# A graph network on one core: edge attributes copied to PSUM ahead of the two statistics scans, and the second block's steps moved

## What is computed

```python
def _gat_layer(x, src, dst, W_i, a_src_i, a_dst_i, b_i):
    h = (x @ W_i).reshape(n, H, C)
    e = leaky_relu(es[src] + ed[dst])
    m = jax.ops.segment_max(e, dst, num_segments=n)
    p = jnp.exp(e - m[dst])
    alpha = p / segment_sum(p, dst)[dst]
    return segment_sum(alpha[:, :, None] * h[src], dst).reshape(n, H * C) + b_i
...
out1 = jax.ops.segment_sum(edge_attr, col, num_segments=n)
mx = jax.ops.segment_max(edge_attr, col, num_segments=n)
...
feat = jnp.concatenate([x, out1, out2, out3, u[batch]], axis=1)
```

## Time and profile before

| | |
|---|---|
| median of 3 runs | 9148.24 us (9145.92 to 9149.09) |
| span of the profiled execution | 9145.7 us |
| gathers of attention layer 1 (first to end of the last) | 2090.0 to 4271.4 us: 2181.4 us |
| layer 2 | 4421.3 to 6602.4 us: 2181.1 us |
| layer 3 (no statistics steps) | 6788.2 to 8929.0 us: 2140.8 us |
| busy share of the span | PE 62%, DVE 59%, POOL 58%, ACT 49% |

### The profile page before, as it was taken

How to read it: one execution, slowest core, us unless ns; L and a number is a source line. 1 busy time by engine, 2 the same in 40 slices (tenths; PEclk the granted TensorE clock), 3 DMA queues, 4 the chain that set the end, 5 groups by cost and what they waited for, 6 DMA issues and landing times.

```text
span 9145.7 us, 130431 instructions
## 1 busy us (share of the span) xinstructions
PE 5627.4 (62%) x34288; PEld 4519.0 (49%) x34288; DVE 5425.3 (59%) x12708; ACT 4499.0 (49%) x8146; POOL 5269.3 (58%) x5192
## 2 busy tenths in 40 slices
PE   4999879974555555555455555555534545445456
PEld 3777646653444454544344545454434444444444
DVE  6888731134666666666466666666645555555555
ACT  2555400014555555554455565555525555555554
POOL 2000100046777777775677777777657777777770
PEclk9999989965555555555555555555555555555558
DMA  3333335504444444443344444444423333333331
GB/s 99 140 139 135 134 131 190 190 8 117 121 118 122 116 125 116 120 119 91 87 121 116 124 116 125 115 121 119 107 64 81 86 81 86 81 86 81 86 81 32
DMA packets 601479, 989.13 MB, mean 108 GB/s; under 512 B 331106, under 2 KB 455043, under 8 KB 561523
## 3 DMA queue, kind: packets, MB, share of 16 engines
q0 software_dynamic: 163760, 357.05, 17.1%
q1 hardware_dynamic: 217540, 544.34, 16.9%
q10 hardware_dynamic: 219648, 81.82, 3.4%
HBM read 758.42 MB, written 224.34 MB: 107 GB/s over the span
## 4 chain that ended last, share of the span: by engine, by line
PE 34%; DVE 18%; DVEq 15%; issue 14%; POOL 13%; DMA 5%; ACT 1%; POOLq 0%; SPq 0%; ACTq 0%
PE bank L979 14%; DVEq L1284 13%; POOL arena L650 12%; PE bank L1202 8%; DVE acc L1882 8%; DMA arena<-row_table,staged_idx 4%; PE bank L1004 3%; PE bank L1130 2%; DVE arena L1838 2%; PE bank L1142 2%; DVEq L1882 1%; DVE arena L1869 1%; DVE x_mem L1556 1%; DVE arena L1831 1%; PE bank L1267 1%
## 5 line engine op out<-in xcount | busy, mean ns | idle before, releaser
L650 POOL DMA_INDIRECT arena<-row_table,staged_idx x4992 | 4982.4, 998 | 1622.7 <-issue 1490.7
L1202 PE MATMUL bank<-arena 128*128 128x136 f32 x9984 | 2504.4, 432 | 1193.0 <-DVE acc L1882 900.5
L1202 PEld LDWEIGHTS bank<-arena 128*128 128x128 f32 x9984 | 2211.2, 318 | 1378.6 <-issue 1372.7
L1882 DVE TENSOR_TENSOR acc<-acc,bank 128x136 f32 x4992 | 1476.6, 296 | 1062.5 <-issue 778.0
L806 ACT ACTIVATE pick_dist<-col,dst_local 128x128 bf16<-128x128 f32 x4992 | 1522.0, 387 | 293.0 <-issue 244.3
L979 PE MATMUL bank<-arena 128*128 128x385 bf16 (+1 forms) x7546 | 1342.6, 327 | 49.5 <-DVE arena L1660 33.0
L598 POOL TENSOR_TENSOR arena<-acc,node_stat 128x896 f32 x14 | 24.4, 1744 | 1730.4 <-POOLq L610 956.4
L1158 PE MATMUL bank<-ident,arena 128*32 128x128 f32 x624 | 161.5, 414 | 1279.5 <-DVE arena L1801 1279.5
L979 PEld LDWEIGHTS bank<-arena 128*128 128x128 bf16 x7546 | 711.7, 98 | 475.9 <-DVE arena L1660 33.2
L1798 DVE TENSOR_TENSOR arena<-arena 128x128 f32<-128x128 f32 x156 | 60.8, 390 | 1320.5 <-DMA arena<-row_table,staged_idx 1320.5
L1869 DVE TENSOR_TENSOR arena<-arena,bank 128x528 f32<-128x528 f32 x1248 | 829.0, 685 | 0.5
(11 more groups left out here) (356 smaller groups left out, 5959.8 us busy)
## 6 DMA issues: line engine op xcount, KB each, us to landing
arena<-dst_rows SPq DMA_DIRECT2D x156, 1024.0 KB, 5.8
cell_rows<-arena SPq DMA_DIRECT2D x76, 1568.0 KB, 5.1
arena<-cell_rows SPq DMA_DIRECT2D x76, 1568.0 KB, 6.5
arena<-row_table,staged_idx POOLq DMA_INDIRECT x4992
edge_stats<-x_mem ACTq DMA_DIRECT2D x416, 192.0 KB
x_mem<-in_edge_attr SPq DMA_DIRECT2D x208, 192.0 KB
x_mem<-segment_flags SPq DMA_DIRECT2D x416, 96.0 KB
arena<-change_rows SPq DMA_DIRECT2D x312, 64.0 KB
```

Of the source, the lines that this page charges most:

```text
L650: pool.indirect_dma_start(gathered[:, at, :], None, table, bass.IndirectOffsetOnAxis(staged_idx[:, at:at + 1], 0)).then_inc(att_gathered[n ...
L1202: mm = pe.matmul(region(k)[:, 0:ROW], pick[:, k, :], gathered[:, b * GROUP + k, :], start=True, stop=True)
L1882: done = dve.tensor_tensor(row, row, region(m * BATCH + k), ALU.add)
```

## The change

Before each pair of scans ACT now copies the block of attributes from SBUF into PSUM bank 0 (`scan_place`, `ea_now`), and both scans read it there. DVE waits for that copy (`st.placed`) in place of the load. The copy waits for the load and for the copies out of bank 0 that came before. The second block's scans go from after batch m = 4 to after m = 6 on DVE; its two `scan_turn` go on PE from m = 6 and 7 to behind `spread_scale` and behind the last scores; its two `scan_copy` go on ACT from round q = 3 to the end of the group.

```diff
--- before.py
+++ after.py
@@ -207,6 +207,7 @@
         ea_flag = x_mem[0:2 * EA, 4 * SCAN:6 * SCAN].bitcast(BF16).rearrange("p (b m e) -> p b m e", b=2, m=2)
         ea_out = x_mem[:, 6 * SCAN:6 * SCAN + 4 * SCAN_CHUNKS * 2 * EA].rearrange(
             "p (b s c w) -> p b s c w", b=2, s=2, c=SCAN_CHUNKS)
+        ea_now = bank[0:2 * EA, 0, 0:SCAN]
         half_of = sb("half_of", [2, 2 * EA], BF16)
         bound = sb("bound", [P, 2], I32)
         bound_f = sb("bound_f", [P, 4])
@@ -353,7 +354,7 @@
                         "summed colvar colroot norm_ready x_done")
         n3 = sems("n3", "scored weights weighed own_ready summed joined elu next turned copied hidden relu "
                         "product added stats_gathered stored")
-        st = sems("stats", "x_kept loaded0 loaded1 scanned turned copied stored0 stored1 carried "
+        st = sems("stats", "x_kept loaded0 loaded1 placed scanned turned copied stored0 stored1 carried "
                            "carry_spread bound_loaded joined x_back")
         att = sems("att", "staged picked rows_loaded turned dst_scored summed added flags0 flags1 "
                           "scored score_rows firsts ends crossed cross_rows maxima max_back shifted prob "
@@ -691,6 +692,13 @@
             def to_xn(t):
                 return xn_flat[:, t * D:(t + 1) * D]
 
+            def scan_place(n, group, q):
+                r = n * (NG * 2) + group * 2 + q
+                act.wait_ge(st_loaded[q], 48 * (n * NG + 1) + group * 48)
+                act.wait_ge(st.copied, r * 2 + 2 * FREE)
+                act.sem_inc(act_tick, 1)
+                nc.scalar.copy(ea_now, ea_in[:, q, :]).then_inc(st.placed, 1)
+
             def keep_turned(s, i):
 
                 act.wait_ge(s.turned, 2 * i + 1 + FREE)
@@ -848,20 +856,22 @@
                     if ahead:
                         stage(1 - b, it + b, it * (2 * GROUP) + (b + 1) * GROUP)
                     for q in range(RNG):
+                        if n < STATS_LAYERS and q == 1:
+                            scan_place(n, g, 0)
                         if n < STATS_LAYERS and q == 2:
                             scan_copy(n, g, 0, 0)
                             scan_copy(n, g, 0, 1)
-                        if n < STATS_LAYERS and q == 3:
-                            scan_copy(n, g, 1, 0)
+                            scan_place(n, g, 1)
                         if head and q == 3:
                             act_exps(n * NG + g + 1, 1 - b)
-                        if n < STATS_LAYERS and q == 3:
-                            scan_copy(n, g, 1, 1)
                         if head:
                             act.wait_ge(att.summed, (n * NG + g + 2) * NBATCH + (q + 1) * (ROUND // BATCH))
                             act_picks(q * ROUND, it * (2 * GROUP) + (b + 1) * GROUP + q * ROUND)
                         if ahead and q < 2:
                             build_pick_t(n * NG + g + 3, q)
+                    if n < STATS_LAYERS:
+                        scan_copy(n, g, 1, 0)
+                        scan_copy(n, g, 1, 1)
 
                 for part_no in range(2):
                     build_pick_t(n * NG + 1, part_no)
@@ -1217,16 +1227,20 @@
                             turn_crossings(G + 1)
                         if head and m == 5:
                             turn_maxima(G + 1)
-                        if n < STATS_LAYERS and m >= 4:
-                            scan_turn(n, g, m // 2 - 2, m % 2)
+                        if n < STATS_LAYERS and m in (4, 5):
+                            scan_turn(n, g, 0, m - 4)
                         if ahead and m == 5:
                             score_some(0, 2, slot, (G + 2) * 2)
                         if ahead and m == 6:
                             score_some(2, 5, slot, (G + 2) * 2)
                     if head:
                         spread_scale(G + 1)
+                    if n < STATS_LAYERS:
+                        scan_turn(n, g, 1, 0)
                     if ahead:
                         score_some(5, QG, slot, (G + 2) * 2)
+                    if n < STATS_LAYERS:
+                        scan_turn(n, g, 1, 1)
 
                 score_some(0, QG, 0, n * NG * 2)
                 turn_scores(n * NG)
@@ -1549,13 +1563,13 @@
 
             def scan_edges(n, group, q):
                 r = n * (NG * 2) + group * 2 + q
-                dve.wait_ge(st_loaded[q], 48 * (n * NG + 1) + group * 48)
+                dve.wait_ge(st.placed, r + 1)
                 dve.wait_ge(st.turned, 2 * r + 2 * FREE)
                 dve.wait_ge(st.scanned, r + FREE)
                 dve.sem_inc(dve_tick, 1)
-                dve.tensor_tensor_scan(ea_max, ea_flag[:, q, 0, :], ea_in[:, q, :], ea_max[:, SCAN - 1:SCAN],
+                dve.tensor_tensor_scan(ea_max, ea_flag[:, q, 0, :], ea_now, ea_max[:, SCAN - 1:SCAN],
                                        ALU.add, ALU.max)
-                dve.tensor_tensor_scan(ea_sum, ea_flag[:, q, 1, :], ea_in[:, q, :], ea_sum[:, SCAN - 1:SCAN],
+                dve.tensor_tensor_scan(ea_sum, ea_flag[:, q, 1, :], ea_now, ea_sum[:, SCAN - 1:SCAN],
                                        ALU.mult, ALU.add).then_inc(st.scanned, 1)
 
             def keep_carry():
@@ -1904,8 +1918,8 @@
                             last_scans(G + 1, 1 - b)
                         if head and m == 5:
                             shift_scores(G + 1, 1 - b, slot + GROUP)
-                        if n < STATS_LAYERS and m in (2, 4):
-                            scan_edges(n, g, m // 2 - 1)
+                        if n < STATS_LAYERS and m in (2, 6):
+                            scan_edges(n, g, m // 4)
 
                 if n == STATS_LAYERS:
                     join_streams()
```

## The result

| | before | after |
|---|---|---|
| median of 4 runs each | 9147.08 us (9143.9 to 9149.09) | 9056.2 us (9054.83 to 9058.38) |
| ratio after/before, 95% interval | | 0.99, 0.9887 to 0.9912 |
| span of the profiled execution | 9145.7 us | 9052.6 us (its own time 9054.83) |

The account below looks back on a forecast made before the run. POOL's gathers, never waiting but some stretched by DVE scans with two SBUF inputs, bound the kernel. 139 - 49 - 5 - 1 = 84 us less gave a 9061.7 us span and a forecast of 9064 us, range 9035 to 9100.

Parts of the forecast that it names:

- The scans read PSUM, 139.1 us: Block's scans in layers 1 and 2 no longer hold gathers such as 8 and 17, removing 69.7 + 69.4 us.
- the third rival: Block's scans reading PSUM still hold gathers, so the time stays at 9148 us, within 10; chance 0.07.
- L1838 catches gather 13, 49 us given back: Gather 13 starts earlier, under a DVE scan with two SBUF inputs; with L1840, 0.47 us a group is lost.
- The new copies: ACT's 208 copies from SBUF to PSUM take 0.58 us each, hidden in ACT's idle time.
- They meet: First block's copy is done at 5225.8, about when DVE is ready for the scan at 5225.85.
- d: DVE's delay waiting for the first block's copy, taken as 0 to 0.1 us; each tenth costs 10 us.
- Second block on DVE, free: Moving the second block's scans from m = 4 to 6 costs nothing; its copy is done well before DVE.
- PE's chain and its cover of 3.4 us: Second turn delays PE's next-group batches 0 and 1 to 5253.4, 3.4 us before gather 0 would wait; no cost.
- The slower rival: PE's late second turn makes gather 0 wait, each microsecond beyond the cover stretching a group by half; 9250 us at 7 late; chance 0.06.
- The tail, 1 to 2 us: At a layer's end one more PE-ACT exchange, DVE waiting in layer 2: 1 to 2 us, once or twice.
- L1838 misses gather 13: Rival: d of 0.55 to 0.8 us puts L1838 behind gather 13's start, holding nothing; 9011 us; chance 0.09.
- Pushed, but not past: Rival: d of 0.2 to 0.5 us pushes L1838 later over gather 13; 9074 to 9106 us; chance 0.12.

Follow-up runs that it names:

- The move alone: Changed kernel with the second block's steps still moved, but no copy and both scans reading SBUF: 9137.82 us, ratio 0.9991 to the kernel before.
- the last segment scans from PSUM: Changed kernel with the last two segment scans also taking their scores from PSUM bank 3, copy L1845 left out: 8966.89 us, ratio 0.98 to the kernel before.
- PSUM alone: Changed kernel with scans reading PSUM but the second block's steps in their old places: 9095.65 us, ratio 0.9942 to the kernel before.
- the experiment: Changed kernel with seven idle ACT activations (7.8 us) ahead of the second block's copies out: 9322.23 us, ratio 1.0188 to the kernel before.

## Why the prediction was right

1. *The scans read PSUM, 139.1 us.* Right in kind and size. No gather is held by L1570 or L1572, and the 69.7 and 69.4 us of holds are gone. The move alone has as many holds as before; with it the third rival (scans still hold, 9148 us) falls. The Trainium skill's "SBUF — State Buffer", section "Who interferes with whom", infers that a `tensor_tensor` does not stall descriptor generation. The 26 gathers under the `tensor_tensor` L1861 disagree, all held, and so do the 784 in the table's two-input rows, under scans. Its other half, no contention with at most one SBUF input, fits all 626 in the one-input rows.
2. *L1838 catches gather 13, 49 us given back.* Right: holds by it went from 1.4 to 25.1 us in layer 1, and there are 26.0 in layer 2, so about 49. Gather 13 takes 1.36 us in the median, and 1.4 was forecast. That this is its whole price is borne out by the last segment scans from PSUM, where layers 1 and 2 get 55 us shorter. (In layer 3 the prediction's 62 us above the gathers' pace should read 63, by its own numbers.)
3. *The new copies.* Interpolated 0.58 us, measured 0.580. "They meet" was a little off on the good side: the copy is done 0.28 us ahead of DVE in the median group, so d is 0, and the 5 us set aside for it and for small operations were not spent.
4. *Second block on DVE, free.* Right, but it is here that the argument had a gap. It costed the move at nothing and did not ask what the old place would have cost with the copy in it: 40 us, by the run with PSUM alone. The two halves of the change are worth 53 and 11 us by themselves and 91 together.
5. *PE's chain and its cover of 3.4 us.* It costs nothing, as said. The batches 0 and 1 end 34.7 us after the landing, 1.5 us earlier than worked out, and gather 0 starts 4.9 us after them. But a gather starts no sooner than 0.82 us after the sums it needs, so the true cover is 4.1 us; the 3.4 of the prediction, by its own numbers, should have been 2.6. The price beyond, half of the excess, was too small as well, by 0.4 to 0.5 us a group in the experiment. The slower rival names a real mechanism, which needs the turn over 4 us later than it is.
6. *The tail, 1 to 2 us.* Hardly there: from the last gather of layer 1 to the first of layer 2 it is 149.9 us before and 150.0 after, from layer 2 to layer 3 185.9 and 186.3.

The forecast of the span, 9061.7 us, was 9.1 us too high: 5 for d and 1 for the tail, not needed, and 4.3 in layer 3 and ahead of layer 1, where the change does nothing and the two executions just differ; 1.2 us went the other way, such as L1810's holds, which rose from 31.5 to 32.3 us in layer 1. With the copy made late, *L1838 misses gather 13* was seen in two groups of three and gave 9027 us; without the 17 and 16 larger holds left (14.8 us) it would be 9012, against the rival's 9011. That match is partly luck: POOL's 16.7 us of waits are not in the rival's price, and they are nearly cancelled by 14 us less of holds under the first segment scan, which are not in it either. *Pushed, but not past* did not occur, and no run that can be compared tests its price.

## What to carry over

Before a stage that runs at the pace of GpSimd's indirect DMAs, look at the length of each of them, not at waits: a few stretched ones, laid beside VectorE's timeline, name the operation to change, and either one operand in PSUM or a shift of 0.6 us takes most of the hold away. When one hold goes, work out the next gather's new start against every other such operation; here a third of the first gain (49 of 139 us) went to it at once. An operand that another engine has to place is free only where that engine is early, so the place of the operation has to move with it, and a cover is counted to the release, here 0.82 us behind the end of the work, and not to the work's end.

## What the runs showed of the hardware

- A VectorE scan with two SBUF inputs holds a gather that starts under it until 0.75 us after the scan's end; with one of them in PSUM it does not (784 of 784 against 0 of 626). A `tensor_tensor` with two SBUF inputs does it too (L1861, 26 of 26).
- A gather that starts just behind such a scan's start is not held (5236.25 beside 5236.22); one at 0.07 us is (gather 17, beside L1558 in the earlier trace rows). Under the segment scans of the faster chips' runs the limit lies near 0.04 us. Under the block's maximum scan it lies later: before, 75 gathers that start up to 0.095 us behind L1556's start are free, and the first that is held starts 0.127 us behind it.
- Order alone, with no work added or removed, moved the kernel by 142 us: DVE's operations and the gathers keep nearly the same distance to each other in most groups, so a shift of 0.62 us counts in each of them.
- One chip ran the kernel before in 10231 us, the others in 9147 to 9150 us, with gathers of the same 0.94 us.
